# Two one-hot builds on the vector engine, from tensor_scalar to scalar_tensor_tensor

## The reference

```python
edge_index = jnp.stack([src, dst])
x = _layernorm(x + _L0_gnn_ref(x, edge_index, ...))
x = _layernorm(x + _L1_gnn_ref(x, edge_index, edge_attr_64, ...))
# layer 0: row, col = src, dst
h = relu(x[row] @ W1[:d] + x[col] @ W1[d:] + b1)
mask = sigmoid(h @ W2 + b2)[:, 0]
w = mask / (segment_sum(mask, row)[row] + 1e-09)
agg = segment_sum(w[:, None] * x[col], row)
out = relu(where(deg > 0, 0.5 * x + 0.5 * agg, x) @ Wl + bl)
# layer 1
h = concat([x[src], x[dst], edge_features]) @ W1 + b1
h = relu(layernorm(h) * ln_g + ln_b)
messages = (h @ W2 + b2) * sigmoid(edge_features @ gate_w + gate_b)
agg = segment_sum(messages, dst)
# then a GRU cell of agg and x
```

## Time and profile before

| | us |
|---|---|
| median of 3 runs | 5620.51 (5617.99 to 5623.52) |
| the profiled execution | 5560.27 |
| its span | 5558.4 |
| DVE busy | 4290.5 (77%) |
| PE busy | 3498.5 (63%) |
| POOL busy | 3363.4 (61%) |
| ACT busy | 1219.8 (22%) |
| edge stage 0, from the first gather to past the last | 589 to 2728 |
| edge stage 1, likewise | 3023 to 5202 |

### The profile page before, as it was taken

How to read it: one execution, slowest core, us unless ns; L and a number is a source line. 1 busy time by engine, 2 the same in 40 slices (tenths; PEclk the granted TensorE clock), 3 DMA queues, 4 the chain that set the end, 5 groups by cost and what they waited for, 6 DMA issues and landing times. The chain is left out here.

```text
span 5558.4 us, 103248 instructions
## 1 busy us (share of the span) xinstructions
PE 3498.5 (63%) x20835; PEld 3129.9 (56%) x20836; DVE 4290.5 (77%) x15613; ACT 1219.8 (22%) x5374; POOL 3363.4 (61%) x3473
## 2 busy tenths in 40 slices
PE   5411455556655556555597777667677767777797
PEld 4411455546555556554475666666666666666564
DVE  8997677777777777777633998988989999989655
ACT  1210000000000000000132433333333333333223
POOL 0001677777777777777401777777777777777310
PEclk9755678886668876778755989998988899888898
DMA  4100444444444444444322444444444444444201
GB/s 124 47 0 17 138 128 128 129 129 127 130 127 129 128 129 127 130 127 129 92 74 73 106 102 102 100 102 100 101 101 101 101 102 101 101 102 101 51 23 59
DMA packets 609828, 558.60 MB, mean 100 GB/s; under 512 B 372594, under 2 KB 475339, under 8 KB 609384
## 3 DMA queue, kind: packets, MB, share of 16 engines
q0 software_dynamic: 133952, 329.07, 21.5%
q1 hardware_dynamic: 475816, 228.86, 16.1%
HBM read 525.30 MB, written 38.57 MB: 101 GB/s over the span
## 5 line engine op out<-in xcount | busy, mean ns | idle before, releaser
L1416 POOL DMA_INDIRECT crows<-c,cols x1664 | 1667.8, 1002 | 510.9 <-issue 494.8
L904 POOL DMA_INDIRECT bxrows<-bx,cols x1664 | 1631.2, 980 | 508.6 <-issue 506.9
L933 PE MATMUL pre<-near,hotT 128*128 x3328 | 746.4, 415 | 951.8 <-DVE hotT L1002 921.7
L933 PEld LDWEIGHTS pre<-near,hotT 128*128 128x128 f32 x3328 | 692.2, 317 | 990.6 <-issue 990.6
L1472 PE MATMUL scattered<-z,hotw 128*128 128x129 f32 x3328 | 578.1, 340 | 446.5 <-DVE hotw L1585 446.3
L1457 PE MATMUL pre<-w1e,efT 128*128 128x129 f32 x3328 | 695.3, 292 | 195.4 <-DVE hotT L1556 190.6
L1472 PEld LDWEIGHTS scattered<-z,hotw 128*128 128x128 f32 x3328 | 521.0, 242 | 494.8 <-issue 466.3
L1457 PEld LDWEIGHTS pre<-w1e,efT 128*128 128x128 f32 x3328 | 533.7, 202 | 250.2 <-DVE h L1549 147.5
L1459 PE MATMUL pre<-near,hotT 128*128 x3328 | 668.3, 284 | 0.0
L988 DVE TENSOR_TENSOR h<-pre,bxrows 128x512 f32<-128x512 f32 x416 | 267.9, 686 | 464.9 <-DMA bxrows<-bx,cols 460.7
L1564 DVE SCALAR_TENSOR_TENSOR z<-h,rstd,ln_g 128x128 f32<-128x128 f32 x1664 | 575.0, 346 | 45.2 <-issue 42.3
(11 more groups left out here) (227 smaller groups left out, 4501.7 us busy)
## 6 DMA issues: line engine op xcount, KB each, us to landing
spread<-place_rows SPq DMA_DIRECT2D x416, 256.0 KB
ef<-in_edge_attr SPq DMA_DIRECT2D x1664, 32.0 KB
bxrows<-bx,cols POOLq DMA_INDIRECT x1664
crows<-c,cols POOLq DMA_INDIRECT x1664
cols<-columns SPq DMA_DIRECT2D x416, 8.0 KB, 1.9
bx<-in_x SPq DMA_DIRECT2D x1, 6250.0 KB
xs<-in_x SPq DMA_DIRECT2D x48, 128.0 KB
bx<-ab SPq DMA_DIRECT2D x48, 128.0 KB, 1.9
```

The costliest lines, as they stand in the source:

```text
L904: pool.indirect_dma_start(out=bx[q][:, k, 0:2 * D], out_offset=None, in_=s.bx[:, :], in_offset=bass.IndirectOffsetOnAxis(ap=cols[q][:, 0, ...
L933: last = nc.tensor.matmul(pre[:, k, :], hotT[par][:, k * P:(k + 1) * P], s.near[:, bass.ds(tiles[k], 1), :], start=True, stop=True)
L1416: pool.indirect_dma_start(out=crows[q][:, k, 0:D], out_offset=None, in_=s.c[:, :], in_offset=bass.IndirectOffsetOnAxis(ap=cols[q][:, 0, k: ...
```

## The change

Each of the four places trades tensor_scalar for scalar_tensor_tensor, with the same two operations or a multiplication by one. What was a scalar for each partition (or nothing) becomes a second tensor operand: a column of one value for each partition, broadcast along the free axis with a step of zero. A new column `s.one` of ones is set once, in the constants stage.

```diff
@@ constants_stage
             dve.tensor_copy(s.part[:, :], s.part_i[:, 0:1])
+            dve.memset(s.one[:, :], 1.0)
@@ edge_stage0, hotT
-                        dve.tensor_scalar(hotT[par][:, :], spread[q][:, :], s.part[:, 0:1], None,
-                                          ALU.is_equal).then_inc(hotT_made, 1)
+                        dve.scalar_tensor_tensor(hotT[par][:, :], spread[q][:, :], s.part[:, 0:1],
+                                                 s.one[:, 0:1].to_broadcast([P, G * P]), ALU.is_equal,
+                                                 ALU.mult).then_inc(hotT_made, 1)
@@ edge_stage0, hotw
-                            last = dve.tensor_scalar(hotw[other][:, k, :], s.lane[:, :],
-                                                     cols[v].bitcast(F32)[:, 1, k:k + 1],
-                                                     mask[:, other, k:k + 1], ALU.is_equal, ALU.mult)
+                            last = dve.scalar_tensor_tensor(hotw[other][:, k, :], s.lane[:, :],
+                                                            cols[v].bitcast(F32)[:, 1, k:k + 1],
+                                                            mask[:, other, k:k + 1].to_broadcast([P, P]),
+                                                            ALU.is_equal, ALU.mult)
@@ edge_stage1: the same two, with spread[q % 2] and with gate[:, par, k:k + 1].to_broadcast([P, P])
@@ program
-        s.lane, s.part = sb("lane", [P, P], F32), sb("part", [P, 1], F32)
+        s.lane, s.part, s.one = sb("lane", [P, P], F32), sb("part", [P, 1], F32), sb("one", [P, 1], F32)
```

More of the change, by code:

```diff
@@ L1555, in steps @@
                             dve.wait_ge(pre_made, g * 2 - 2)
-                        dve.tensor_scalar(hotT[par][:, :], spread[q % 2][:, :], s.part[:, 0:1], None,
-                                          ALU.is_equal).then_inc(hotT_made, 1)
+                        dve.scalar_tensor_tensor(hotT[par][:, :], spread[q % 2][:, :], s.part[:, 0:1],
+                                                 s.one[:, 0:1].to_broadcast([P, G * P]), ALU.is_equal,
+                                                 ALU.mult).then_inc(hotT_made, 1)
                     if has(g, 3):
@@ L1584, in steps @@
                         for k in range(G):
-                            last = dve.tensor_scalar(hotw[par][:, k, :], s.lane[:, :],
-                                                     cols[v].bitcast(F32)[:, 1, k:k + 1],
-                                                     gate[:, par, k:k + 1], ALU.is_equal, ALU.mult)
+                            last = dve.scalar_tensor_tensor(hotw[par][:, k, :], s.lane[:, :],
+                                                            cols[v].bitcast(F32)[:, 1, k:k + 1],
+                                                            gate[:, par, k:k + 1].to_broadcast([P, P]),
+                                                            ALU.is_equal, ALU.mult)
                             if k % 4 == 3:
```

## The result

The changed kernel took 5779.75 us in the median of 4 runs (5759.61 to 5809.32); the kernel before, run beside it and earlier, 5619.25 (5566.51 to 5623.52, 4 runs). The medians are 160 us apart. The ratio on record, which isn't that of the two medians, is 1.0364, with a 95% interval of 1.0303 to 1.0424: slower, by some 204 us on 5620. The profiled execution took 5797.89, span 5796.1, where the one of before had 5558.4: 238 us more.

What follows compares the result with a forecast made beforehand. POOL's back-to-back gathers were taken to pace both edge stages. Terms 110 (hotT, stage 0) + 98 (hotT, stage 1) + 12 (hotw) = 220, rounded to 215, put on the median 5620.51, gave 5835 us; range 5755 to 5890.

Steps and rivals of the forecast that it cites:

- hotT's length: On DVE in both stages: hotT goes from 0.74 to 1.28 us, plus 0.54 us.
- Stage 0, +110: Edge stage 0: the gather under each longer hotT waits 0.53 us more, times 208 groups, 110 us.
- The 0.48 and 0.68 places: Stage 0: how many us into hotT the gather comes; predicted extra waits there of 0.54 and 0.52 us.
- Stage 1, +98: Edge stage 1: gathers under hotT wait 0.54 or 0.34 us more, 0.47 x 208 = 98 us.
- hotw, +12: Both stages, eight hotw a group in each: gathers held 0.03 us a group longer, 12 us.
- rival 3: Stage 1: slower period makes gathers come late in hotT; price falls from 98 to 42 or 20, about 5765; chance 0.10.
- The cover that I counted for DVE: Stage 1: DVE's wait for POOL's gathered rows, 0.7 us a group, taken to absorb longer DVE work.
- the row of line 1564: Profile row of a 128x128 scalar_tensor_tensor, two SBUF inputs, 346 ns; taken as hotw's model, with little gather loss.
- rival 4: Stage 1: eight back-to-back hotw hold one or two gathers, +0.35 x 208 = 73 us on top, 5908; chance 0.08.
- The sum: Both stages: 110 + 98 + 12 = 220 us, rounded down to 215, giving 5835 on the median.
- What would show it: Signs listed beforehand, such as gather means near 1046 and 1062 ns, or against: POOL waiting over 30 us in stage 1.

Runs made afterwards that it cites:

- The PSUM column: The kernel before with stage 0's hotT as scalar_tensor_tensor, its column of ones in PSUM: ratio 0.9949, 28 us faster.
- the four quarters: The changed kernel with each hotT split into four instructions of 256 columns: ratio 1.0074 to the kernel before.
- the fastest kernel: The kernel before with hotT as scalar_tensor_tensor, ones in PSUM in stage 0, in SBUF in stage 1: ratio 0.9806, median 5491.36 against 5586.86.

## Why the prediction was right, point by point

- *What bounds the kernel.* Right: all but 13 of the 238 us lie in the gathers of the two stages, and POOL gained no idle time.
- *hotT's length.* 1.28 predicted, 1277 and 1276 ns.
- *A gather is held until a two-input instruction in SBUF ends.* Right for hotT. The PSUM column shows that it is the input and not the length, and the four quarters that it is one instruction's end. In a run of eight hotw it is not the whole truth: there a late gather mostly waits past the end of its own instruction.
- *Stage 0, +110.* The stage gained 109 in the profile, hotT alone 101. The 0.48 and 0.68 places came back to 0.01 us. Of the 110 us that the gathers lost more, hotT took 90 and hotw 23, where I had 110 and 6.
- *Stage 1, +98, and hotw, +12.* The stage gained 116 with both, but not by these terms: in the trace hotT takes 74 more, hotw 105 more, and the other lines 61 less, which the sum had at nothing. hotT alone made the stage 60 us shorter, and no rival had that: rival 3 let the stage settle elsewhere, but at +20 us or more. The cover that I counted for DVE (0.7 us a group) was itself a wait that set where DVE meets the gathers. When hotT used it up, the meeting moved and most gathers fell between the holding instructions. I had written that if the cover were gone it would cost 0.54 a group; it gained instead. hotw was mis-sized: 12 us for both stages, 33 + 43 measured alone. I took the row of line 1564 for it, which alternates with line 1574, an instruction that hardly holds (0.01 us a group); back to back the late ones hold together. That is rival 4, to which I gave 0.08: its price was 0.35 a group, in the trace it is 0.50 (0.53 less 0.03). With hotw changed too, gathers get slower, DVE waits for rows again (237 us), and hotT costs 0.35 more a group.
- *The sum.* 220, rounded to 215; 238 in the profiled executions, about 204 by the ratio, 160 between the medians. That it fits is luck in good part. The terms were 208 for hotT, 12 for hotw and nothing for the rest; the traces show 164, 128 and -64, and these happen to add up to 228. The forecast of 5835 lies 55 above the median, the ratio on 5620.51 would give 5825.
- *The Trainium skill* (SBUF — State Buffer, Who interferes with whom) infers that a two-input instruction doesn't stall descriptor generation; the runs disagree, with gathers of 1.74 us under such a hotT, and 0.95 once one input lay in PSUM. That the section has a two-input instruction contend with GpSimd's reads would fit, if what a gather needs 0.12 us after its start is to read its indices; no run here shows what it is.
- *What would show it.* The means (1046 predicted, 1046 measured; 1062 and 1073) and the wait for rows over 2 us a group (2.7) held. One gather a group at 1.55 to 1.75 us didn't come so: in stage 0 188 of 208 take 1.50 to 1.85 under hotT, in stage 1 only 57. POOL waiting for DVE over 30 us in stage 1 was named as a sign against, and it was 34.7; but that is 114 waits of at most 0.3 us, no longer than the issue time ahead of any gather, so it can't be told from it.

## What to carry to other kernels

When an engine's queue issues gathers back to back, look for the long instructions on the vector engine that hold them (here those with two SBUF inputs, and for less time tensor_scalar), and put the timelines of both side by side: where one instruction holds a gather, the gather's extra time ends where that instruction ends, as it did under hotT. Here splitting that instruction, or taking one of its inputs out of SBUF, won the time back, though neither made the vector engine's work shorter. A small wait that recurs each round can be what sets an unlucky meeting of two engines; adding or moving a few tenths of a microsecond tests that, and terms worked out one by one don't add up where two engines keep step like this.

## What the runs showed of the hardware beyond that

The kernel before takes about 5560 or about 5620 us: of 17 runs on one chip six took 5554 to 5564, eight 5617 to 5644, and three some 5586. Of the profiled executions on chips where the kernel before takes these times, two fell in the longer kind, hotw alone and the fastest kernel, with their first gather at 648 and 649 us where the others have 587 to 589: some 60 us are lost in the sort, ahead of both stages, in one wait. In the fastest kernel:

```profile
DVE keys_even L276 <- ACT keys_odd L343: 72.0, 7, 63.8
```

In the traces with the early first gather that line's waits sum to 9 us. What the stall is stays open.

A tensor_scalar can itself be held by a gather. In stage 1 of the kernel before, the 76 hotT that start 0.5 to 0.7 us after a gather's start take 0.77 to 0.96 us in place of 0.74 (one is in the earlier trace rows). The two-input hotT isn't held there: with hotT alone changed, the 49 that start as late take 1272 to 1276 ns, and in the changed kernel all 416 take 1270 to 1334.
